# Attention and feed-forward block on one core: the softmax division moves from the probability rows to the attention output

## The reference, cut to what matters

```
qkv = layernorm(x) @ w_qkv.T            # x: 1024 tokens x 512
scores = q @ k.T * 128**-0.5            # 32 query heads of 128, 8 key/value heads, causal mask
probs = softmax(scores)
attn = (probs @ v) @ w_dense.T
x = x + layernorm(attn)
# feed forward on layernorm(x): quantised per token and 128 columns,
y = (silu(xq @ w1.T) * (xq @ w3.T)) quantised again, @ w2.T
x = x + layernorm(y)
```

## Time and profile before

| | us |
|---|---|
| median of 3 runs (1142.47 to 1144.24) | 1142.49 |
| span of the profiled execution, first to last instruction | 1140.7 |
| what lies around the span (median less span) | 1.8 |
| TensorE busy in the span | 1122.7 |
| DVE, ACT, POOL busy | 833.9, 626.1, 713.9 |

### The profile page before, as it was taken

The page is one execution under the profiler, slowest core; times in us unless marked ns, Lnnn a source line. Parts: engine busy times, 40 slices in busy tenths (PEclk is TensorE's granted clock), DMA queues, the critical chain, the costliest instruction groups (busy, mean ns, idle before and its releaser), DMA issues.

```text
span 1140.7 us, 17840 instructions
## 1 busy us (share of the span) xinstructions
PE 1122.7 (98%) x5512; PEld 945.5 (83%) x5512; DVE 833.9 (73%) x1987; ACT 626.1 (55%) x1350; POOL 713.9 (63%) x802
## 2 busy tenths in 40 slices
PE   8999999999999999999999999999999989999997
PEld 7888888888888888888888888888887768888885
DVE  5645454557888898888888888988579766666666
ACT  6532324237776767676767767776588532222224
POOL 7844447436674865856757748567784746665645
PEclk9999999999999999999999999999999999999999
DMA  6443555335466475485474665754410033333422
GB/s 224 138 158 148 184 203 185 148 128 183 129 194 218 152 224 183 142 265 173 143 262 127 206 205 159 240 172 121 167 65 1 20 115 114 109 111 92 121 65 98
DMA packets 154696, 173.76 MB, mean 152 GB/s; under 512 B 41776, under 2 KB 128496, under 8 KB 151280
## 3 DMA queue, kind: packets, MB, share of 16 engines
q1 hardware_dynamic: 154608, 172.68, 46.8%
HBM read 101.06 MB, written 71.57 MB: 151 GB/s over the span
## 4 chain that ended last, share of the span: by engine, by line
PE 93%; DVE 2%; POOL 2%; ACT 1%; issue 1%; DMA 0%; POOLq 0%; DVEq 0%; SPq 0%; ACTq 0%
PE psS L1813 29%; PE psOY L1942 17%; PE psOY L1957 15%; PE psOY L1813 15%; PE psT L1813 11%; PE psT L1920 5%; POOL x L1100 0%; DVE pT_lo L1468 0%; PE psS L1819 0%; POOL raw_up L1000 0%; DMA raw<-in_w_v 0%; DVE y L1612 0%; POOL rstd L1031 0%; POOL up_lo L896 0%; DVE probs_long L1533 0%
## 5 line engine op out<-in xcount | busy, mean ns | idle before, releaser
L955 POOL TENSOR_SCALAR probs_long<-probs_long,rsum 128x896 f32<-128x896 f32 (+9 forms) x124 | 129.0, 1042 | 62.3 <-DVE rsum L1539 60.9
L1269 ACT ACTIVATE probs_long<-probs_long,negmax 128x896 f32<-128x896 f32 (+9 forms) x124 | 121.4, 979 | 42.0 <-DVE negmax L1533 39.7
L955 POOL TENSOR_SCALAR probs_short<-probs_short,rsum 128x416 f32<-128x416 f32 (+15 forms) x128 | 69.0, 543 | 120.1 <-DVE rsum L1539 119.7
L1813 PE MATMUL psS<-kT_hi,qT_hi 128*128 128x256 f32 (+8 forms) x384 | 133.0, 346 | 0.0
L1813 PE MATMUL psS<-kT_hi,qT_lo 128*128 128x256 f32 (+8 forms) x384 | 128.3, 334 | 0.0
L1813 PE MATMUL psS<-kT_lo,qT_hi 128*128 128x256 f32 (+8 forms) x384 | 128.1, 334 | 0.0
L1957 PE MATMUL psOY<-wd_hi,oT_hi 128*128 128x512 f32 x256 | 106.8, 417 | 3.3 <-DVE oT_lo L1468 3.3
L1022 POOL TENSOR_SCALAR hidden<-mask,hr,hs 128x128 f32<-128x128 f32 x112 | 50.0, 456 | 86.2 <-DVE hr L1632 82.1
L1957 PE MATMUL psOY<-wd_hi,oT_lo 128*128 128x512 f32 x256 | 101.2, 395 | 0.0
L1957 PE MATMUL psOY<-wd_lo,oT_hi 128*128 128x512 f32 x256 | 100.5, 393 | 0.0
L1264 ACT CAST pT_hi<-square 128x1024 fp32r<-128x1024 f32 (+3 forms) x87 | 77.6, 892 | 31.6 <-DVE square L1552 31.2
(11 more groups left out here) (200 smaller groups left out, 3267.1 us busy)
## 6 DMA issues: line engine op xcount, KB each, us to landing
q_raw<-q_scr SPq DMA_DIRECT2D x64, 256.0 KB, 3.4
p_scr<-probs_long SPq DMA_DIRECT2D x24, 512.0 KB, 3.3
raw<-in_w_qk SPq DMA_DIRECT2D x10, 1024.0 KB, 5.6
p_scr<-probs_long SPq DMA_DIRECT2D x21, 448.0 KB, 2.5
probs_long<-p_scr SPq DMA_DIRECT2D x90, 96.0 KB, 2.8
q_scr<-cB SPq DMA_DIRECT2D x16, 512.0 KB, 2.6
q_scr<-cA SPq DMA_DIRECT2D x16, 512.0 KB, 2.7
raw_wd<-in_w_dense SPq DMA_DIRECT2D x8, 1024.0 KB, 8.4
```

Source lines behind the costliest of these rows:

```text
L955: nc.gpsimd.tensor_scalar(row, row, rsum[:, column(t, h)], 1.0, ALU.mult, ALU.mult).then_inc(p_ready, 1)
L1269: nc.scalar.activation(row, row, ACT.Exp, bias=negmax[:, column(t, h)], scale=-1.0, accum_out=lsum[:, column(t, h)]).then_inc(e_done, 1)
L1813: last = nc.tensor.matmul(dst, a, b, start=(start and k == 0), stop=(stop and k == len(terms) - 1), skip_group_check=resumed)
```

## The change

`norm_head` is gone, and with it one inverse per head. The sums of the four heads of a step go to one row of `lsum`, and one `reciprocal` makes four inverses (`inverse_sums`). They lie one per query partition, but the attention output has the queries along its columns. So SP writes them to HBM (`inverses_away`, item `RA`) and reads them back with the same 512 numbers in every partition (`inverses_back`, item `RB`). At the output DVE multiplies `psO` by them into a new buffer `o_sb` (`scale_output`), ACT rounds that to `oT_hi`, and POOL subtracts to `oT_lo` (`lo_of_output`). `psO` is now free after the multiplication (`o_scaled`), and `o_done`, for which the output product waits, comes after POOL. Rows are transposed, or sent to HBM, right after the exponential. SP's transfers get a list of items and a table of their own, and all the tables are new; which units are exchanged stays as it was. The lists hold the same items as before on each engine.

```diff
+            def inverses_away(t):
+                sp.wait_ge(r_done, t + 1)
+                sp.dma_start(r_scr[t % INVERSES], rsum[:, t % INVERSES, :]).then_inc(r_out[t % INVERSES], 16)
+
+            def inverses_back(t):
+                sp.wait_ge(r_out[t % INVERSES], 16 * (t // INVERSES + 1))
+                if t >= 2:
+                    sp.wait_ge(o_scaled, t - 1)
+                sp.dma_start(inverses[t % 2][:], r_scr[t % INVERSES].rearrange("p u -> (p u)").unsqueeze(0).broadcast_to(
+                    [P, BANK])).then_inc(r_in[t % 2], 16)
...
-            def norm_head(t, h):
-                pool.wait_ge(r_done, softmax_count(t, h))
-                row = whole_row(t, h)[:, 0:keys_of(t, h)]
-                if h < HG - 1 and swapped(t - 2, h) and not swapped(t, h):
-                    nc.gpsimd.memset(probs_long[:, h, S - SPAN * (HG - 1 - h):S], 0.0).then_inc(const_ready, 1)
-                nc.gpsimd.tensor_scalar(row, row, rsum[:, column(t, h)], 1.0, ALU.mult, ALU.mult).then_inc(p_ready, 1)
+            def lo_of_output(t):
+                pool.wait_ge(o_hi, t + 1)
+                low(oT[1][:], o_sb[:], oT[0][:]).then_inc(o_done, 1)
...
                 elif kind == "O":
-                    act.wait_ge(o_full, args[0] + 1)
-                    nc.scalar.copy(by_head(oT[0]), from_units(psO)).then_inc(o_hi, 1)
+                    act.wait_ge(o_scaled, args[0] + 1)
+                    if args[0] >= 1:
+                        act.wait_ge(y_full, args[0])
+                    nc.scalar.copy(oT[0][:], o_sb[:]).then_inc(o_hi, 1)
...
-            def inverse_sum(t, h):
-                dve.wait_ge(e_done, softmax_count(t, h))
-                nc.vector.reciprocal(rsum[:, column(t, h)], lsum[:, column(t, h)]).then_inc(r_done, 1)
+            def inverse_sums(t):
+                dve.wait_ge(e_done, LAST_SCORE[t] + 1)
+                if t >= INVERSES:
+                    dve.wait_ge(r_out[t % INVERSES], 16 * (t // INVERSES))
+                nc.vector.reciprocal(rsum[:, t % INVERSES, :], lsum[:, t % LANES, :]).then_inc(r_done, 1)
+
+            def scale_output(t):
+                dve.wait_ge(o_full, t + 1)
+                dve.wait_ge(r_in[t % 2], 16 * (t // 2 + 1))
+                if t >= 1:
+                    dve.wait_ge(o_done, t)
+                inverse = inverses[t % 2][:].rearrange("p (b q u) -> p b u q", b=HG, u=HG)
+                nc.vector.tensor_tensor(by_head(o_sb), from_units(psO), inverse, ALU.mult).then_inc(o_scaled, 1)
...
                 if b == 0:
-                    pe.wait_ge(p_ready, softmax_count(t, h))
+                    pe.wait_ge(e_done, softmax_count(t, h))
...
-                        pe.wait_ge(o_done, t)
+                        pe.wait_ge(o_scaled, t)
...
-    PE_LATER = {("DN",): 4.8, ("GU",): -1.2, ("X",): 0.6, ("P", -8, 0, 0): 3, ("P", -8, 0, 2): -1.2, ("PV", -8, 0): 0,
+    PE_LATER = {("DN",): 96.4, ("GU",): -2.4, ("X",): 0.6, ("P", -8, 0, 0): -18, ("P", -8, 0, 1): -93.6,
```

More of the change, by code:

```diff
@@ L271, in in_order @@
                 *ATTENTION[end:]]
+    LOADS_IN_ORDER = []
+    for t in range(2, T):
+        if t - 3 in SWAPPED:
+            away = swaps(t - 3)
+            LOADS_IN_ORDER += [("SA", t - 3, away[0]), *[item for k in range(1, len(away)) for item in (
+                ("SA", t - 3, away[k]), ("SB", t - 3, away[k - 1]))], ("SB", t - 3, away[-1])]
+            LOADS_IN_ORDER += [("RA", t - 3), ("RB", t - 3), ("LQ", t)]
+        else:
+            LOADS_IN_ORDER += [("LQ", t)] + [item for k in {3: (0,), 4: (1,), 2: ()}.get(t, (t - 3,)) for item in (("RA", k), ("RB", k))]
+        if t % NT == 4 and t // NT + 1 < G:
+            LOADS_IN_ORDER += [("LKV", t // NT + 1), ("LD", t // NT + 1)]
+        if t == T - NT + 2:
+            LOADS_IN_ORDER.append(("LC",))
+        if t == T - NT + 3:
+            LOADS_IN_ORDER.append(("LX",))
+    LOADS_IN_ORDER += [(kind, t) for t in range(T - 3, T) for kind in ("RA", "RB")]
     TURN = {item: k for k, item in enumerate(item for item in ATTENTION if item[0] == "P")}
@@ L553, in sandwich_kernel @@
         junk = [at(f"junk{e}", 64 + 2 * e, [P, D]) for e in range(2)]
+        inverses = [at(f"inverses{e}", (132, 146)[e], [P, BANK]) for e in range(2)]
+        o_sb = at("o_sb", 148, [P, BANK])
         oT = [at(f"oT_{p}", 72 + 2 * n, [P, BANK], F32R) for n, p in enumerate(PARTS)]
@@ L692, in whole_row, with row_of, before_in_row, lane @@
             return buffer[:, u, n - (TILES[t] + 1) * P:n]
+        def row_of(t):
+            return "mid" if t == T - 2 else TILES[t] >= TPB
+        def before_in_row(t):
+            return max((k for k in range(t) if row_of(k) == row_of(t)), default=None)
         def column(t, u):
             return slice(SOFT[t, u] % (2 * HG), SOFT[t, u] % (2 * HG) + 1)
+        def lane(t, u):
+            return lsum[:, t % LANES, u:u + 1]
+        def refilled(t, u):
+            return u < HG - 1 and t >= 2 and swapped(t - 2, u) and not swapped(t, u)
+        def refills(t, u):
+            return sum(refilled(k, w) for k, w in SOFT if SOFT[k, w] <= SOFT[t, u])
         def squared(t, u):
@@ L1733, in _ @@
                 elif kind == "O":
[L1734 to L1735 removed]
+                    scale_output(*args)
                 elif kind == "X":
```

114 lines of the change are left out of this document (70 added, 44 removed), and 401 rows, old and new, of tables (ACT_LATER, DVE_LATER, PE_LATER, POOL_LATER).

## The result

The changed kernel takes 1210.38 us (median of 4 runs, 1206.27 to 1214.12), the kernel before 1142.56 us beside it: a ratio of 1.0589 [1.0565, 1.0614], 67.8 us slower. The forecast was 1144.3, with a range of 1138 to 1149.

What follows compares the result with a forecast made beforehand. The prediction took TensorE, busy for 1122.7 of 1140.7 us, to bound the kernel. Its terms were 1142.5 + 1.3 + 1.8 - 0.1 - 1.2 = 1144.3 us, with a range of 1138 to 1149.

Steps and rivals of the forecast that it cites:

- Each stands there after its data are due, and the ones behind it (exchanged units, queries) are some us ahead of their use, so nothing.: SP's queue: the 128 added transfers of the inverses' round trip delay nothing behind them; cost nothing.
- rival of late inverses: SP's queue: a transfer behind a blocked one makes inverses late; over 1155 us, chance 0.05.
- 0.20 to the start.: Output chain: DVE's product starts 0.20 us after the last value matmul gives up its slot; chain 2.94 us in all.
- late output chain: Rival, output chain: DVE is at something else when the values end, so the chain is later; about 1150 us, chance 0.14.
- I take 0.69, the nearest row: Output chain: DVE's product of `psO` and an SBUF tile takes 0.69 us, like the subtraction of that shape.
- I cost this at nothing: Steady stretch: removing POOL's row multiplications and three of four DVE inverses gains nothing, since no TensorE wait ends at them.
- The output product before the next rounding (`y_full`) is long done in each place.: Output chain: ACT's next rounding never has to wait for the previous output product; no cost.
- -1.2 us: Tail, step 62's values to the 7th tile's gate matmuls: 35.8 us after the change, 37.0 before.
- no drop of the clock: Tail: no fall to the lower clock level is counted, since DVE's pace hides most of one.
- So TensorE waits some 0.22 us: Output chain at t = 7, 15, ..., 47: chain of 2.94 us against 2.69 to 2.72 of work; six times, +1.3 us.
- +1.8 us: Output chain where TILES is 3: POOL's subtraction waits for DVE's low part, TensorE waits 0.3 us, six times.
- TensorE has no wait in the steady groups: Sign, steady groups: seeing no TensorE wait there would show the prediction wrong; it expected small waits.

Runs made afterwards that it cites:

- e10: Changed kernel with old inverses at the outputs; 128 transfers of the same size still issued, but nothing waits for them: 1197.19 us, 1.0493.
- e2: Changed kernel without the inverses' way through HBM after the first two steps, so outputs use the inverses of step 0 or 1: 1194.15 us, 1.0449.
- e4: Changed kernel with the edits of e1, e2 and e3 together: 1172.18 us, 1.0252.
- e1: Changed kernel with DVE reading adjacent inverses, not every fourth, so outputs are scaled by another query's inverse: 1202.53 us, 1.0523.
- e8: Kernel before, in its old order, with only POOL's row multiplications left out: 1142.86 us, 0.9999.
- e3: Changed kernel with POOL's subtractions for queries, keys and values made one-input multiplications by one: 1201.24 us, 1.0527.
- e6: e4 with two buffers each for the rounded output and its low part, so ACT waits for the output product before the last: 1160.15 us, 1.0144.
- e5: e4 with POOL's low part of the output made from one input (a copy), not by a two-input subtraction: 1154.49 us, 1.0091.
- e7: e4 with the edits of e5 and e6 together: 1161.20 us, 1.0154.
- e15: Changed kernel with e5's edit alone, POOL's low part of the output a one-input multiplication: 1204.93 us, 1.0528.

## Why the prediction was wrong

It looked at each item by itself and at its own place; what decided was how they hold one another back: a standing queue, DVE's list, and an output chain behind both. By its own steps:

- **"Each stands there after its data are due, and the ones behind it (exchanged units, queries) are some us ahead of their use, so nothing."** This is the step that failed. I took the new transfers to be issued once their data are due, and didn't lay the list of SP against the trace. `RA` and `RB` stood 82.5 us; 25 rows were late by 31.9 us. Taking the waits away gives 13 us back (e10), the whole round trip 16 (e2). The rival of late inverses had the blocked queue and a price of "each us beyond the margin", but for inverses, for which DVE waited once, 0.2 us; the rows behind them were late. This step explains some 16 of the 67.8 us; the next ones have the rest.
- **"0.20 to the start."** The chain was priced from the values' end. At even steps DVE was 0.5 to 3.9 us late, since its list has the turn of an exchanged row, and often more, first. The sum of the chain itself was right: in e4, where the product takes 0.69, the output product of step 31 starts 2.97 us after the values, forecast 2.94. The rival "late output chain", 1150 with a chance of 0.14, had the mechanism, DVE at something else when the values end, and that is what 27 of the 47.0 us of lateness are; but it priced it in tenths of a us and had no wait for a row. By my count those waits make the steps late where TILES is 3; there the forecast had 0.3 us each, and TensorE stood idle for 1.25 to 2.58.
- **"I take 0.69, the nearest row."** It is 1.07, well inside the bounds of 0.59 and 1.29, so the value was chosen too near the lower one; e1 makes it 0.69 and gives 7.9 us. The only difference is the step of 16 bytes between two inverses that it reads. The Trainium skill ("SBUF — State Buffer", section "Door 1: The DMA port swizzle (why `[64,N]` ≈ `[32,N]`)") says that SBUF has 16-byte lines and that each access that crosses to a new one pays; the trace agrees, with 0.38 us for 512 columns.
- **"I cost this at nothing"** (POOL's removed work) held: e8. But in the new order POOL's subtractions fell beside DVE's. The lock was weighed with POOL as the second, at six places, for 1.8 us. With DVE as the second it cost 27.4 us of DVE's time, and e3, which makes the queries', keys' and values' subtractions light, gives 9.1. At step 24, the place where it was forecast, the mechanism is there: POOL's subtraction takes 1.55 us.
- **"The output product before the next rounding (`y_full`) is long done in each place."** ACT waited for it 26.4 us in 18 waits; on e4, two buffers give 12.0 (e6), on e5 nothing (e7). In the new order step t - 1's output product stands behind step t's values at several places, and that hadn't been counted.
- **"-1.2 us" for the tail.** It was +4.7. That DVE sets the pace and that step 62's output is waited for less was right. The 28.2 us from step 63's values to the 7th tile's gates were short by 4.5 (they began 32.7 us after, 980.31 less 947.6), and "no drop of the clock" was wrong: these matmuls ran at the lower level.
- **"So TensorE waits some 0.22 us", six times, and "+1.8 us".** These are terms of the right mechanism, but below one tenth of the 52 us of standstills. One sign of being wrong was that "TensorE has no wait in the steady groups": it has many, only far larger ones.

The causes don't add up one by one: the same edit helps by 5.5 us in the changed kernel (e15) and by 17.7 with the other three causes out (e5). I read this as one loop, a late row, a late product, a late score, a late row; no run opened it at a single place, so the loop is argued and not shown. Of the 67.8 us, 38.2 go with the round trip, the stepped read and the locks of the queries', keys' and values' low parts, and 17.7 with the two-input low part of the output. The last 11.6 us, e5 against the kernel before, stay open: the traces put some 5 in the tail, some 5 in steady standstills and 4 in small pieces (15 us between the two profiled executions, since e5's took 3.0 us more than its median), and no run took these apart. The order of items was never tried alone, without a new chain. But e5 has the whole new order and products that are late by 29.1 us over the same even steps, and it loses only these 11.6 us in all: most of that lateness is hidden once the chain behind it is short. No version found here beats the kernel before.

## What to carry to other kernels

When a change adds a transfer that waits to a queue in order, price it by what stands behind it, with the trace's own times at which each item's data are ready, and ask of every engine in order what it holds back when its next item is late. Where DVE reads two inputs from SBUF and POOL reads there too, relieving one of them moves its work in time, possibly beside the other's, so count the overlaps both ways. If several small costs delay one another around a nearly full TensorE, no sum of tenths is a bound: one removed alone may give little (5.5 us here), and much more once the others are gone (17.7).

## What the runs showed of the hardware

A store of 512 pieces of 4 bytes to HBM landed in 9.3 us in the median, one of 128 pieces of 16 bytes in 2.8, for the same 2 KB. Reading 256 KB from a source of 2 KB landed in 4.4 us, no faster than 256 KB of queries (4.7). Issuing a transfer held POOL for 0.56 us (the store) and 0.55 (the read) in the median. A DVE product whose SBUF input has a step of 16 bytes took 1.07 us, with adjacent numbers 0.69. When a two-input operation of DVE and an operation of POOL overlapped, the second one, whichever it was, took longer by about their overlap less 0.13 us; this was so for POOL's two-input subtractions, and in e5 also for its one-input copy.
